# A four-layer cross-attention kernel: the latent layers' output projection in whole fp32 operands

## The chip, the core and the metric

The kernel runs on one core of one Trainium2 chip. Its time is the device time of one execution in microseconds (us); lower is better. A core has five engines that run their own instruction streams and meet at semaphores: TensorE (PE; its weight loads are listed as PEld), VectorE (DVE), ScalarE (ACT), GpSimd (POOL) and SyncE (SP), which here issues all DMAs.

## What is computed

Four attention layers run one after the other on 16 batches of a 128 x 512 fp32 activation. Layers 0 and 3 are the "latent" kind, layer 1 is grouped-query attention, layer 2 is cross attention. All but layer 1 end in an MLP of width 2048. A latent layer, cut to what matters (here `h` is the context and the latents together, 16 heads of 32):

```python
q  = latents @ q_w + q_b
kv = h @ kv_w + kv_b
attn = softmax(where(mask, q @ k.T / 32, -inf))
attn_out = attn @ v                          # (16, 128, 512)
attn_out = attn_out @ out_w + out_b + residual   # the output projection
out = rmsnorm(attn_out, postnorm_w)
out = gelu(out @ mlp_w1 + mlp_b1) @ mlp_w2 + mlp_b2
return out + residual
```

The change is in the line marked as the output projection, in layers 0 and 3.

## The kernel before

**Split operands.** Dense products are made from fp32r operands (a rounded fp32 type that TensorE takes as it is). Each operand is held twice: `hi` is the value rounded to fp32r, `lo` is the fp32r of value minus `hi`. `three_passes` (recorded as L326) multiplies lo x hi, hi x lo and hi x hi into the same bank of PSUM, so one product of 128 rows of contraction takes three matmuls. A few products take plain fp32 operands instead: attention times values in `pe_attend` (L497), and the transposes (L467, L361, L521).

**Where operands lie.** On-chip memory is seen through two sets of tensors over the same bytes: `plain_low`, `plain_high`, `plain_work` in fp32, and `rounded_low`, `rounded_high`, `rounded_work` in fp32r. Slots 0 to 7 are "low", 8 to 15 "high". Layer 0's output weight has slots 6 and 7 (hi and lo, low) and its heads slot 15 (high); layer 3's has slots 14 and 15 (high) and its heads slot 7 (low). So in a trace the output projection of layer 0 is `banks<-rounded_low,rounded_high` and that of layer 3 `banks<-rounded_high,rounded_low`, each 192 matmuls.

**Weights.** SP loads a weight in tiles of 128 x 512 (`load_tile`) into a double buffer, and POOL splits each with `split_tile`: a cast to `hi` (L315), then a subtraction to `lo` (L317). Layer 0's four output-weight tiles are split right at the start; layer 3's are the last four of 16 that POOL splits during the last group of layer 2's MLP.

**Banks.** PSUM has 8 banks. Four hold scores or MLP sums. The other four are a ring (`begin`): every result takes the next one and waits until the reader of four results ago has counted its `evac` semaphore.

**A latent layer.** Batches go in 8 pairs `p`, each with four rounds `k` (batch k % 2, heads half k // 2). The orders on the engines are written out by hand in `pe_latent`, `act_latent`, `dve_latent`, `pool_latent`, `sp_latent`. For a middle pair PE runs: scores(p,1), transposes of the probabilities of (p,0), **out(2p-1)**, attend(p,0), keys 0 and 1 of pair p+1, scores(p,2), transposes(p,1), queries 0, attend(p,1), values, scores(p,3), transposes(p,2), keys 2, attend(p,2), keys 3, scores(p+1,0), transposes(p,3), **out(2p)**, attend(p,3), queries, values. out(15) stands alone behind the last pair. So each of the two layers has 16 output projections ("out blocks"): eight out(2p), seven out(2p-1), and out(15).

**Around an out block.** `pe_attend` leaves a round's heads in a ring bank. `act_heads` (L745) writes bias plus value of two 128 x 128 blocks as `hi`; `dve_heads` (L1053) then writes the two `lo` blocks and frees the bank. `pe_out` waits for the bank's `evac` of the two rounds of its batch, and multiplies four blocks of heads (as weights) by the output weight (512 columns, moving). `dve_out` (L1150) adds it to the residual in `hidden`, then come statistics (L1135, L1137, L1140) on DVE, the root and the scaling on POOL (`pool_root`), and a store by SP. In layer 0 the keys of pair p+1 wait for that pair's inputs: ACT rounds them (`act_stage`, L809) after the exponentials of heads 0 and 1 of scores(p,1), DVE makes the `lo` part (`dve_stage`, L1109) and counts `xc_ready`.

Of the kernel before, what the change touches and what calls it, by code (L numbers as in the profile page):

```python
# [8 lines left out]
ACT = mybir.ActivationFunctionType  # L9
# [7 lines left out]
P = 128  # L17
B = 16
PAIRS = B // 2
D = 512  # L20
FB = D // P
# [7 lines left out]
LATENT, GQA, CROSS = "latent", "gqa", "cross"  # L29
# [33 lines left out]
def build(nc, ins, out):  # L63
# [9 lines left out]
    with ctx:  # L73
# [3 lines left out]
        def sem(name):  # L77
            return ctx.enter_context(nc.semaphore(name))

        C_KB = 76  # L80
        with nc.sbuf_tensor("plain_low", [P, 8 * 2048], F32) as plain_low, \
                nc.sbuf_tensor("plain_high", [P, 8 * 2048], F32) as plain_high, \
                nc.sbuf_tensor("plain_work", [P, C_KB * KB], F32) as plain_work:
            plain = [plain_low, plain_high, plain_work]
# [3 lines left out]
        def shaped(v, shape):  # L88
            names = "abcd"[:len(shape)]
            if len(shape) == 1:  # L90
                return v
            return v.rearrange(f"p ({' '.join(names)}) -> p {' '.join(names)}", **dict(zip(names[1:], shape[1:])))

        def work(t, at_kb, *shape):
            at, n = int(at_kb * KB), int(np.prod(shape))
            return shaped(t[2][:, at:at + n], shape)

        def slots(t, s, *shape):
            at, n = (s % 8) * 2048, int(np.prod(shape))
            return shaped(t[s // 8][:, at:at + n], shape)  # L100
# [35 lines left out]
        def prob(y):  # L136
            return [slots(plain, y.probs + h, 4, D) for h in range(2)]

        def prob_t(y):
            return work(plain, 36, 4, D) if y.kind == GQA else slots(plain, y.probs + 2, 4, D)  # L140

        def heads_t(y):
            return slots(rounded, 15 if y.kind == GQA else y.probs + 3, 2, 2, 4, P)

# [58 lines left out]
        raw_scaled, tile_hi, tile_split = sem("raw_scaled"), sem("tile_hi"), sem("tile_split")  # L203
# [9 lines left out]
        def bank(key):  # L213
            return PS[:, 4 + ring[key] % 4, :]

        def begin(pe, key):
            n = len(ring)
            ring[key] = n
            wait(pe, evac[n % 4], n // 4)
            return PS[:, 4 + n % 4, :]  # L220

        def filled_by(key):
            return filled[ring[key] % 4]

        def evac_of(key):
            return evac[ring[key] % 4]

        def wait_filled(eng, key):
            eng.wait_ge(filled[ring[key] % 4], ring[key] // 4 + 1)

        def wait_evac(eng, key):
            eng.wait_ge(evac[ring[key] % 4], ring[key] // 4 + 1)
# [10 lines left out]
        def col(y, i):  # L243
            return cols[:, y.n, i:i + 1]

        def of_round(y, k):
            return (k, 0) if y.kind == CROSS else (k % 2, k // 2)
# [24 lines left out]
        def attention_tiles(y, names):  # L272
            t = []
            a = ins[f"attention_w{y.n}"]
            if "kv" in names:
                for f in range(FB):
                    t.append((ins["attention_kv1"][f], 2 * P, W[10][:, f * 256:f * 256 + 256], W[10][:, 1024 + f * 256:1024 + f * 256 + 256], None))
            for name in [n for n in names if n != "kv"]:
                hi, lo = y.homes[name]
                for f in range(FB):  # L280
                    t.append((a[("qo" if y.kind == GQA else "kvqo").index(name), f], D, W[hi][:, f * D:(f + 1) * D], W[lo][:, f * D:(f + 1) * D],
                              y.scale if name == "q" else None))
            return t
# [23 lines left out]
        def split_tile(pool, key, i):  # L307
            n = first_tile[key] + i
            src, width, hi, lo, scale = tile_table[key][i]
            buf = raw[:, n % 2, 0:width]  # L310
            pool.wait_ge(raw_loaded[n % 2], 16 * (n // 2 + 1))
            if scale is not None:
                pool.tensor_scalar(buf, buf, scale, 1.0, ALU.mult, ALU.mult).then_inc(raw_scaled, 1)
                pool.wait_ge(raw_scaled, scale_order.index((key, i)) + 1)
            pool.tensor_copy(hi, buf).then_inc(tile_hi, 1)  # L315
            pool.wait_ge(tile_hi, n + 1)
            pool.tensor_tensor(lo, buf, hi.bitcast(F32), ALU.subtract).then_inc(tile_split, 1)  # L317
# [6 lines left out]
        def three_passes(pe, dst, lhs, rhs, first, last):  # L324
            for n, (i, j) in enumerate(((1, 0), (0, 1), (0, 0))):
                mm = pe.matmul(dst, lhs(i), rhs(j), start=first and n == 0, stop=last and n == 2, skip_group_check=True)  # L326
            return mm
# [131 lines left out]
        def pe_turn_probs(pe, y, p, k):  # L459
            R = y.round(p, k)  # L460
            pr = prob(y)[R % 2]
            for r in range(4):
                key = ("T", R, r)
                dst = begin(pe, key)
                pe.wait_ge(normed, 4 * R + r + 1)
                for t in range(4):
                    mm = pe.transpose(dst[:, t * P:(t + 1) * P], pr[:, r, t * P:(t + 1) * P], ident[:, :])  # L467
                mm.then_inc(filled_by(key), 1)

        def pe_attend(pe, y, p, k):  # L470
            R = y.round(p, k)
            b, s = of_round(y, k)
            pt = prob_t(y)
            key = ("O", R)
            dst = begin(pe, key)
            for r in range(4):
                wait_evac(pe, ("T", R, r))
            if y.kind == CROSS:
                pe.wait_ge(vc_loaded[p % 2], 16 * (p // 2 + 1))
            else:  # L480
                for i in range(4 if y.kind == LATENT else 1):
                    wait_evac(pe, ("V", y.n, p, i))
            n_blk = 4 if y.kind == CROSS else 2
            n_t = 4 // n_blk
            for i in range(n_blk):
                c = n_blk * s + i
                for t in range(n_t):
                    for r in range(4):
                        u = 4 * c + r
                        if y.kind == LATENT:  # L490
                            v = V_L[p % 2][:, 2 * t + b, 32 * u:32 * u + 32]
                        elif y.kind == GQA:
                            v = V_G[p % 2][:, 4 * b + r, t, :]
                        else:
                            v = V_C[p % 2][:, b, 32 * u:32 * u + 32]
                        at = (i * n_t + t) * P
                        mm = pe.matmul(dst[32 * r:32 * r + 32, i * P:(i + 1) * P], v, pt[:, r, at:at + P],  # L497
                                       start=t == 0, stop=t == n_t - 1, skip_group_check=True)
            mm.then_inc(filled_by(key), 1)

        def pe_out(pe, y, b):
            if b == 0:
                pe_weights(pe, y, "o")
            p = b // 2
            for k in range(y.per_pair):
                if of_round(y, k)[0] == b % 2:
                    wait_evac(pe, ("O", y.round(p, k)))
            key = ("out", y.n, b)
            dst = begin(pe, key)
            ot = heads_t(y)  # L510
            for f in range(FB):
                mm = three_passes(pe, dst, lambda h: ot[:, b % 2, h, f, :], lambda h: weight(y, "o", h, f, 0, D), f == 0, f == FB - 1)
            mm.then_inc(filled_by(key), 1)
# [222 lines left out]
        def act_heads(act, y, p, k):  # L736
            R = y.round(p, k)
            b, s = of_round(y, k)
            key = ("O", R)
            ot = heads_t(y)  # L740
            n_blk = 4 if y.kind == CROSS else 2
            wait_filled(act, key)
            for i in range(n_blk):
                c = n_blk * s + i
                last = act.activation(ot[:, b, 0, c, :], bank(key)[:, i * P:(i + 1) * P], ACT.Identity, bias=col(y, 8 + c))  # L745
            last.then_inc(hi_done, hi_count(key))

        def act_keys(act, y, p, i):
# [293 lines left out]
                dve_invert(dve, y, p, k)  # L1042

        def dve_heads(dve, y, p, k):
            R = y.round(p, k)
            b, s = of_round(y, k)
            key = ("O", R)
            ot = heads_t(y)
            n_blk = 4 if y.kind == CROSS else 2
            wait_hi(dve, key)  # L1050
            for i in range(n_blk):
                c = n_blk * s + i
                last = dve.scalar_tensor_tensor(out=ot[:, b, 1, c, :], in0=bank(key)[:, i * P:(i + 1) * P], scalar=col(y, 8 + c),  # L1053
                                                in1=ot[:, b, 0, c, :].bitcast(F32), op0=ALU.add, op1=ALU.subtract)
            last.then_inc(evac_of(key), 1)
# [913 lines left out]
```

## Time and profile before

| | |
|---|---|
| time, median of 2 runs | 2566.01 us (2565.93 to 2566.09) |
| the profiled execution's own time | 2566.45 us |
| its span, first to last instruction | 2564.5 us |
| PE busy | 2450.6 us (96%), 18464 matmuls |
| DVE / ACT / POOL busy | 1235.5 / 1085.5 / 1118.6 us (48 / 42 / 44%) |
| mean granted TensorE clock | 0.983 of full |
| HBM read, written | 136.22 MB, 58.72 MB: 76 GB/s over the span |

The profile is one execution. A row of a group gives the line of the source, engine, operation, what is written from what, the shape, the count, then busy time and mean length of one, and idle time before it with what ended it. Matmuls are pipelined: the length of one overlaps the next, so the cost of a matmul in a stream is the time of a run of them divided by their count, not its own length. The chain of work that ended last gives such runs. From the activations of the MLPs the stages are: layer 0 to 448 us, its MLP to 792, layers 1 and 2 to 1431, MLP to 1775, layer 3 to 2210, MLP to the end.

### The profile page before, as it was taken

The page shows a single profiled execution, that of the slowest core. Times are in us where ns is not written, and L with a number is a line of the kernel's source. Part 1 is how long each engine was busy: PE and PEld are TensorE (multiplying, and loading weights), DVE is VectorE, ACT ScalarE, POOL GpSimd, SP SyncE. Part 2 cuts the span into 40 slices and gives each one's busy share as a digit, 9 for nine tenths or more (in the row PEclk, how much of TensorE's full clock was granted, in tenths as well). Part 3 has the DMA queues.
Part 4 walks back from the last instruction along what each step waited for, and adds up shares of the span by engine and source line. Part 5 has one row for each costly group of instructions (what it writes and reads, how often), then busy time and mean ns, then how long its engine had stood idle before and what let it go on. Part 6 is the DMA issues. An engine that isn't in the chain of part 4 may idle for free.

```text
span 2564.5 us, 48767 instructions
## 1 busy us (share of the span) xinstructions
PE 2450.6 (96%) x18464; PEld 2052.2 (80%) x18464; DVE 1235.5 (48%) x3296; ACT 1085.5 (42%) x3712; POOL 1118.6 (44%) x1972
## 2 busy tenths in 40 slices
PE   7999998999999999998888999999999999899999
PEld 6888786888888878886777788888888888788887
DVE  4555655333234666766666442333455555432332
ACT  4555555111113777787676211111555555311111
POOL 2444435600043787878876740023344443730000
PEclk9999999999999999998998999999999999999999
DMA  4111222311034223223453320122022111320100
GB/s 162 59 59 59 96 63 67 95 50 50 1 98 136 74 106 120 90 102 124 137 168 120 116 96 1 50 84 77 26 84 66 51 42 59 116 87 1 50 33 17
DMA packets 106774, 198.07 MB, mean 77 GB/s; under 512 B 8304, under 2 KB 35632, under 8 KB 103600
## 3 DMA queue, kind: packets, MB, share of 16 engines
q1 hardware_dynamic: 106544, 194.97, 22.8%
q8 instruction: 149, 2.44, 0.4%
q14 instruction: 81, 0.66, 0.1%
HBM read 136.22 MB, written 58.72 MB: 76 GB/s over the span
## 4 chain that ended last, share of the span: by engine, by line
PE 79%; ACT 11%; DVE 5%; POOL 3%; issue 1%; DMA 1%; SPq 0%; DVEq 0%; POOLq 0%
PE banks L326 70%; ACT plain_high L731 5%; PE banks L467 5%; PE banks L497 3%; ACT plain_low L731 2%; POOL plain_high L1344 2%; ACT plain_work L796 1%; DVE stats L1135 1%; PE banks L521 1%; DVE rounded_work L1109 1%; ACT plain_work L715 1%; DMA plain_high<-attention_w 0%; DVE plain_work L1150 0%; DVE plain_high L1004 0%; ACT plain_low L715 0%
## 5 line engine op out<-in xcount | busy, mean ns | idle before, releaser
L326 PE MATMUL banks<-rounded_work,rounded_low 128*128 128x512 f32 (+1 forms) x2688 | 536.8, 356 | 18.9 <-DVE rounded_low L1168 9.5
L326 PEld LDWEIGHTS banks<-rounded_work,rounded_low 128*128 128x128 f32 x2688 | 447.4, 200 | 84.4 <-issue 12.3
L982 ACT ACTIVATE plain_work<-banks,columns 128x512 f32<-128x512 f32 x192 | 132.4, 690 | 870.8 <-PE banks L326 870.8
L326 PE MATMUL banks<-rounded_work,rounded_high 128*128 128x512 f32 (+1 forms) x2400 | 480.9, 354 | 1.0 <-DMA rounded_work<-ctx_split 0.6
L326 PEld LDWEIGHTS banks<-rounded_work,rounded_high 128*128 128x128 f32 x2400 | 394.3, 190 | 66.7 <-issue 5.8
L1344 POOL TENSOR_SCALAR plain_high<-plain_high,inv_sum 128x128 f32<-128x128 f32 (+1 forms) x768 | 296.1, 408 | 324.2 <-DVE inv_sum L1026 323.8
L1320 DVE CAST rounded_work<-plain_work 128x512 fp32r<-128x512 f32 x192 | 105.7, 551 | 683.2 <-ACT plain_work L982 672.5
L326 PE MATMUL banks<-rounded_low,rounded_work 128*128 128x512 f32 x1728 | 414.9, 391 | 0.0
L326 PE MATMUL banks<-rounded_high,rounded_work 128*128 128x512 f32 (+1 forms) x1728 | 390.2, 377 | 0.0
L326 PEld LDWEIGHTS banks<-rounded_low,rounded_work 128*128 128x128 f32 x1728 | 321.6, 188 | 68.6 <-issue 2.8
L326 PEld LDWEIGHTS banks<-rounded_high,rounded_work 128*128 128x128 f32 x1728 | 309.1, 188 | 60.6 <-issue 1.4
L1344 POOL TENSOR_SCALAR plain_low<-plain_low,inv_sum 128x128 f32<-128x128 f32 (+1 forms) x512 | 218.7, 448 | 283.1 <-DVE inv_sum L1026 283.0
L1490 POOL TENSOR_TENSOR plain_work<-plain_work 128x512 f32<-128x512 f32 x48 | 66.6, 1418 | 609.4 <-DMA plain_work<-x 417.1
L731 ACT ACTIVATE plain_low<-banks,neg_max 128x128 f32<-128x128 f32 (+1 forms) x512 | 208.9, 456 | 27.9 <-DVE neg_max L1008 27.9
L731 ACT ACTIVATE plain_high<-plain_high,neg_max 128x128 f32<-128x128 f32 x512 | 198.1, 392 | 33.5 <-DVE neg_max L1004 33.5
L1008 DVE TENSOR_REDUCE neg_max<-banks 128x2 f32<-128x512 f32 (+1 forms) x320 | 204.9, 683 | 14.0 <-PE banks L456 13.9
L467 PE MATMUL banks<-ident,plain_high 128*128 128x128 f32 x1024 | 139.1, 284 | 28.4 <-POOL plain_high L1344 22.5
L1322 DVE TENSOR_TENSOR rounded_work<-plain_work,rounded_work 128x512 fp32r<-128x512 f32 x192 | 162.0, 844 | 6.6
L467 PEld LDWEIGHTS banks<-ident,plain_high 128*128 128x128 f32 x1024 | 112.5, 143 | 47.7 <-issue 25.8
L1026 DVE RECIPROCAL inv_sum<-row_sum 128x4 f32<-128x4 f32 (+1 forms) x224 | 41.7, 187 | 219.8 <-ACT plain_high L731 124.9
L326 PEld LDWEIGHTS banks<-rounded_work 32*128 32x128 f32 x3072 | 101.3, 185 | 43.0 <-issue 41.1
L326 PE MATMUL banks<-rounded_work 32*128 32x256 f32 (+1 forms) x3072 | 123.1, 289 | 9.7 <-DVE rounded_work L1080 7.0
(106 smaller groups left out, 3120.6 us busy)
## 6 DMA issues: line engine op xcount, KB each, us to landing
plain_work<-x SPq DMA_DIRECT2D x96, 256.0 KB, 3.2
plain_work<-mlp_w SPq DMA_DIRECT2D x96, 256.0 KB, 2.7
rounded_work<-ctx_split SPq DMA_DIRECT2D x16, 1024.0 KB, 6.0
u<-plain_work SPq DMA_DIRECT2D x48, 256.0 KB, 2.7
plain_work<-u SPq DMA_DIRECT2D x12, 1024.0 KB, 7.1
x<-plain_work SPq DMA_DIRECT2D x48, 256.0 KB, 2.3
plain_work<-attention_w SPq DMA_DIRECT2D x44, 256.0 KB, 2.7
ctx_split<-rounded_work SPq DMA_DIRECT2D x8, 1024.0 KB, 5.6
```

The costliest lines, as they stand in the source:

```text
L326: mm = pe.matmul(dst, lhs(i), rhs(j), start=first and n == 0, stop=last and n == 2, skip_group_check=True)
L467: mm = pe.transpose(dst[:, t * P:(t + 1) * P], pr[:, r, t * P:(t + 1) * P], ident[:, :])
L497: mm = pe.matmul(dst[32 * r:32 * r + 32, i * P:(i + 1) * P], v, pt[:, r, at:at + P], start=t == 0, stop=t == n_t - 1, skip_group_check=True)
L521: mm = pe.transpose(dst[:, r * P:(r + 1) * P], u_nat[:, r, f * P:(f + 1) * P], ident[:, :])
L731: last = act.activation(pr[:, r, part], pr[:, r, part] if gqa else PS[:, r, part], ACT.Exp, scale=-1.0 if gqa else 1.0, bias=neg_max[:, R ...
L982: act.activation(gelu[:, j % 2, :], bank(key), ACT.Gelu_apprx_tanh, bias=col(y, 28 + j)).then_inc(evac_of(key), 1)
L1008: dve.tensor_reduce(neg_max[:, R % 2, r, 0:y.segs], src.rearrange("p (g n) -> p g n", g=y.segs), AX.X, ALU.max, negate=True).then_inc(maxe ...
L1026: dve.reciprocal(inv_sum[:, R % 2, 2 * half:2 * half + 2, 0:y.segs], row_sum[:, R % 2, 2 * half:2 * half + 2, 0:y.segs]).then_inc(inverted, 1)
L1320: dve.tensor_copy(G[:, j % 4, 0, :], gelu[:, j % 2, :]).then_inc(g_hi, 1)
L1322: dve.tensor_tensor(G[:, j % 4, 1, :], gelu[:, j % 2, :], G[:, j % 4, 0, :].bitcast(F32), ALU.subtract).then_inc(g_ready, 1)
L1344: last = pool.tensor_scalar(part, part, inv_sum[:, R % 2, r, g:g + 1], 1.0, ALU.mult, ALU.mult)
L1490: last = pool.tensor_tensor(res[:, r, :], res[:, r, :], wide_bias, ALU.add)
```

## The change

In the two latent layers the output projection takes plain fp32 operands. `pe_out` issues one fp32 matmul for each of the four blocks instead of three fp32r ones. `act_heads` writes the heads as fp32 and frees the bank itself; `dve_heads` returns at once. `split_tile` copies the weight tile in two halves (the second one counts the semaphore that the subtraction counted) and makes no `lo`. Layers 1 and 2 are as before.

```diff
+        def full_heads_t(y):
+            return slots(plain, y.probs + 3, 2, 4, P)
 ...
             for name in [n for n in names if n != "kv"]:
                 hi, lo = y.homes[name]
                 for f in range(FB):
+                    if y.kind == LATENT and name == "o":
+                        t.append((a["kvqo".index(name), f], D, slots(plain, hi, 2048)[:, f * D:(f + 1) * D], None, None))
+                        continue
 ...
         def split_tile(pool, key, i):
+            if lo is None:
+                half = width // 2
+                pool.tensor_copy(hi[:, 0:half], buf[:, 0:half]).then_inc(tile_hi, 1)
+                pool.tensor_copy(hi[:, half:width], buf[:, half:width]).then_inc(tile_split, 1)
+                return
             pool.tensor_copy(hi, buf).then_inc(tile_hi, 1)
             pool.wait_ge(tile_hi, n + 1)
             pool.tensor_tensor(lo, buf, hi.bitcast(F32), ALU.subtract).then_inc(tile_split, 1)
 ...
             ot = heads_t(y)
+            if y.kind == LATENT:
+                full, w = full_heads_t(y), slots(plain, y.homes["o"][0], FB, D)
+                for f in range(FB):
+                    mm = pe.matmul(dst, full[:, b % 2, f, :], w[:, f, :], start=f == 0, stop=f == FB - 1, skip_group_check=True)
+                mm.then_inc(filled_by(key), 1)
+                return
             for f in range(FB):
                 mm = three_passes(pe, dst, lambda h: ot[:, b % 2, h, f, :], lambda h: weight(y, "o", h, f, 0, D), f == 0, f == FB - 1)
 ...
-                last = act.activation(ot[:, b, 0, c, :], bank(key)[:, i * P:(i + 1) * P], ACT.Identity, bias=col(y, 8 + c))
+                to = full_heads_t(y)[:, b, c, :] if y.kind == LATENT else ot[:, b, 0, c, :]
+                last = act.activation(to, bank(key)[:, i * P:(i + 1) * P], ACT.Identity, bias=col(y, 8 + c))
+            if y.kind == LATENT:
+                last.then_inc(evac_of(key), 1)
+                return
             last.then_inc(hi_done, hi_count(key))
 ...
         def dve_heads(dve, y, p, k):
+            if y.kind == LATENT:
+                return
```

On PE, around an out block of layer 0 in the order of issue (rows of the program: names as above, shape and count; L497 is attend, L467 the transposes). Before:

```order
L326 MATMUL banks<-rounded_work 128x256 x24
L456 MATMUL banks<-plain_work,ones_row 128x2x128 x4
L467 MATMUL banks<-ident,plain_high 128x128 x16
L326 MATMUL banks<-rounded_low,rounded_high 128x512 x12
L497 MATMUL banks<-plain_high,plain_work 32x128 x16
L326 MATMUL banks<-rounded_work,rounded_low 128x256 x24
```

and now, with the lines of the changed kernel:

```order
L337 MATMUL banks<-rounded_work 128x256 x24
L467 MATMUL banks<-plain_work,ones_row 128x2x128 x4
L478 MATMUL banks<-ident,plain_high 128x128 x16
L525 MATMUL banks<-plain_low,plain_high 128x512 x4
L508 MATMUL banks<-plain_high,plain_work 32x128 x16
L337 MATMUL banks<-rounded_work,rounded_low 128x256 x24
```

The twelve matmuls of an out block are four; nothing else changes place. On DVE, from an out block's sum to the next exponentials' maxima, before:

```order
L1150 TENSOR_TENSOR plain_work<-banks,plain_work 128x512
L1135 BN_STATS stats<-plain_work 128x6
L1137 BN_AGGR moments<-stats 128x2
L1140 SCALAR_TENSOR_TENSOR spread<-moments 128x1
L1053 SCALAR_TENSOR_TENSOR rounded_high<-banks,columns,rounded_high 128x128 x2
L1080 SCALAR_TENSOR_TENSOR rounded_work<-banks,columns,rounded_work 128x256 x2
```

and now:

```order
L1173 TENSOR_TENSOR plain_work<-banks,plain_work 128x512
L1158 BN_STATS stats<-plain_work 128x6
L1160 BN_AGGR moments<-stats 128x2
L1163 SCALAR_TENSOR_TENSOR spread<-moments 128x1
L1103 SCALAR_TENSOR_TENSOR rounded_work<-banks,columns,rounded_work 128x256 x2
```

The two instructions that made the `lo` heads (old L1053) are gone there, as they are after every attend of layers 0 and 3.

## Rows read from the trace of the kernel before

**Rows 1.** The page, part 1: busy us, share of span, count.
```profile
PE 2450.6 (96%) x18464; PEld 2052.2 (80%) x18464; DVE 1235.5 (48%) x3296; ACT 1085.5 (42%) x3712; POOL 1118.6 (44%) x1972
```

**Rows 2.** The page, part 4: shares of the chain that ended last, by engine.
```profile
PE 79%; ACT 11%; DVE 5%; POOL 3%; issue 1%; DMA 1%; SPq 0%; DVEq 0%; POOLq 0%
```

**Rows 3.** Busy time by stage: layer 0, its MLP, layer 3.
```profile
core 0: us, PE busy (x) PEld busy (x) DVE busy (x) ACT busy (x) POOL busy (x), PEclk, DMA share, GB/s
26.00:448.30 422.30, 401.49 (x3727) 333.11 (x3726) 237.57 (x483) 226.60 (x734) 187.53 (x350) 0.98 0.21 66
448.30:791.60 343.30, 343.30 (x1540) 284.95 (x1540) 103.68 (x150) 51.37 (x76) 100.57 (x98) 1.00 0.19 61
...
1774.60:2210.40 435.80, 422.69 (x3902) 351.82 (x3901) 241.46 (x498) 226.35 (x744) 184.91 (x347) 0.99 0.19 63
```

**Rows 4.** Groups by form, whole program, PE and PEld: xcount | busy us, mean ns.
```profile
L326 PE MATMUL banks<-rounded_low,rounded_high 128*128 128x512 f32 x192 | 48.3, 400 | 1.5 <-issue 1.5
...
L497 PE MATMUL banks<-plain_high,plain_work 128*32 128x128 f32 x1024 | 34.9, 277 | 3.7 <-DVE plain_high L1013 2.2 <-issue 1.5
...
L326 PEld LDWEIGHTS banks<-rounded_low,rounded_high 128*128 128x128 f32 x192 | 35.2, 190 | 8.6 <-issue 1.8
...
L497 PEld LDWEIGHTS banks<-plain_high,plain_work 128*32 128x32 f32 x1024 | 26.3, 110 | 13.2 <-issue 12.2
```

**Rows 5.** Chain that ended last, pair 3 of layer 0: start us, us, what.
```profile
202.94 0.60 ACT plain_high L715
...
205.85 0.96 ACT rounded_work L809
...
207.97 1.23 DVE rounded_work L1109
...
209.24 6.70 PE banks L326 x48
215.94 0.13 PE banks L456 x4
216.07 1.90 PE banks L467 x16
217.96 2.87 PE banks L326 x24
220.84 1.01 PE banks L497 x32
...
230.50 2.75 PE banks L326 x12
```

**Rows 6.** Waits of PE in layer 0: us in total, times, longest us.
```profile
PE banks L326 <- DVE rounded_work L1109: 9.3, 7, 1.7
```

**Rows 7.** Timeline of PE and DVE, last pair of layer 0: out(13) and what follows.
```profile
410.72 0.84 PE L326 MATMUL banks<-rounded_low,rounded_high 128*128 128x512 f32 x3
411.50 1.08 PE L497 MATMUL banks<-plain_high,plain_work 128*32 128x128 f32 x32
...
424.52 3.81 PE L467 MATMUL banks<-ident,plain_high 128*128 128x128 f32 x16 [3.37 <-POOL plain_high L1344]
```

**Rows 8.** Chain that ended last, last pair of layer 0.
```profile
412.47 0.70 DVE plain_work L1150
...
416.58 2.89 DMA plain_work<-mlp_w
```

**Rows 9.** Timeline of layer 3's last pair: out(13) and its sum.
```profile
2171.53 2.99 PE L326 MATMUL banks<-rounded_high,rounded_low 128*128 128x512 f32 x12
...
2175.43 0.69 DVE L1150 TENSOR_TENSOR plain_work<-banks,plain_work 128x512 f32<-128x512 f32 x1
```

**Rows 10.** Timeline between the last attend of layer 0 and out(15).
```profile
441.08 0.62 ACT L745 ACTIVATE rounded_high<-banks,columns 128x128 fp32r<-128x128 f32 x2 [4.36 <-PE banks L497]
...
441.85 0.60 DVE L1053 SCALAR_TENSOR_TENSOR rounded_high<-banks,columns,rounded_high 128x128 fp32r<-128x128 f32 x2
...
442.56 1.17 PE L326 MATMUL banks<-rounded_low,rounded_high 128*128 128x512 f32 x4 [1.54 <-issue]
```

**Rows 11.** Groups on DVE in layer 0, the heads' second parts.
```profile
L1053 DVE SCALAR_TENSOR_TENSOR rounded_high<-banks,columns,rounded_high 128x128 fp32r<-128x128 f32 x64 | 19.2, 342 | 0.3 <-ACT rounded_high L745 0.3
```

**Rows 12.** POOL's subtraction (L317) by tile: ns min/median/max, starts, forms.
```profile
L317 POOL TENSOR_TENSOR rounded_low<-plain_work,rounded_low x68: 1262/1288/3266, 17.7 to 2247.2; 128x512 fp32r<-128x512 f32 x68
```

## The prediction

> **What bounds the kernel now.** I read the page's busy times first: PE is busy 96% of the span, no other engine over 48% [rows 1]. The chain that ended last agrees: 79% of it is PE [rows 2]. Busy time by stage then says where the change falls. The two latent layers hold 422 and 436 us, of which PE lacks about 21 and 13 us; in the MLP behind layer 0 it lacks nothing [rows 3]. So in these layers a longer or shorter PE block is a longer or shorter kernel, except where PE waits anyway right behind it. Work taken from DVE or POOL is worth something only where PE waits for just that work. The chain of one pair of layer 0 shows both: long unbroken runs of PE, and one place where the chain leaves PE for ACT and DVE [rows 5].
>
> **What an out block costs now.** Its twelve fp32r matmuls of 512 columns, between transposes and attend, take 2.75 us in the chain [rows 5], 229 ns each. Its group has 192 of them in layer 0, so 16 blocks [rows 4]; layer 3 has the same number under swapped names. That is 32 blocks and 88 us in all.
>
> **What it costs afterwards.** The trace has no plain fp32 matmul of 512 columns, so this price is built from the nearest rows.
> - How many instructions: the program issues 16 matmuls in an attend, and the trace has 32 MATMULs for it [rows 5]. So one plain fp32 matmul runs as two MATMULs, each with its own weight load (1024 of each in layer 0 for 32 rounds [rows 4]). An out block becomes 8 MATMULs.
> - How long each: the 32 MATMULs of an attend, 128 columns each, take 1.01 us. They use 32 weight columns each and lie four abreast in the array, so they are eight steps of some 109 ns with a bit of filling (1.01 / 8 = 126 at most). The fp32r stream of 24 with 256 columns takes 2.87 us, 120 ns each [rows 5]. A plain fp32 MATMUL of 128 columns thus needs about what an fp32r one of 256 needs: it streams its columns twice. The transposes say the same: 16 of 128 columns in 1.90 us, 119 ns each with the draining of the last one in it [rows 5]. And the mask's four bf16 matmuls of 256 columns, four abreast, take 0.13 us [rows 5], as long as one such step of 128 fp32 columns.
> - So a MATMUL of 512 plain columns should cost four times a step of 128. Below: two fp32r streams less their fixed part. fp32r goes from 120 ns at 256 columns to 229 at 512, 109 ns for 256 more columns, so 1024 columns take 4 x 109 = 436 ns, or 447 with the 11 ns that the 256-column row has over 109. Above: twice the whole 229, 458 ns. I take 436 to 447, rounded to 440, as the plain matmuls of the attend show no more than 109 for their step. The block: 8 x 440 = 3.52 us, 0.77 us more than 2.75.
> - The Trainium skill ("FP8 and Floating Point Precision", TensorE Precision Notes) says that true fp32 is four passes through the array. By that rule and the 229 ns of an fp32r pass a block would be 16 x 229 = 3.66 us, 0.91 more instead of 0.77; summed as below that would give 2586 instead of 2583. The rows on the attend agree with the four passes.
>
> **Where the 0.77 us is hidden.** In layer 0, out(2p-1) is followed by attend(p,0) and then by the keys of the next pair, and these wait for the inputs: 7 waits of 9.3 us in all, the longest 1.7 [rows 6]. The longest is pair 0, which has no out before it; the other six (p = 1 to 6) have 1.27 us each. The chain there runs ACT's copy of the transposes, exponentials, L809, DVE's L1109 [rows 5], and needs nothing of the out block. So the six blocks grow into a wait of 1.27 us and cost nothing; half a microsecond of it stays. A seventh is out(13) of layer 0: what follows it waits at the next transposes 3.37 us for POOL [rows 7], whose chain goes through DVE's sum L1150 of out(13) at 412.47 [rows 8], while the block ends at 410.72 + 0.84 = 411.56 [rows 7]. The slack of 0.91 covers 0.77. An eighth is the same block in layer 3: it ends at 2171.53 + 2.99 = 2174.52, DVE takes it up at 2175.43 [rows 9], slack 0.91. The other 24 blocks (16 - 7 and 16 - 1) have no such wait near them and stand on PE's path.
>
> **What is saved.** DVE loses 128 instructions of 342 ns, 44 us [rows 11], layer 3 as layer 0. No PE wait in the steady pairs is for them, so this cover costs nothing and brings nothing, with one exception in each layer: out(15) waits for the last heads. There ACT works 0.62 us from 441.08, DVE from 441.85 to 442.45, PE starts at 442.56 [rows 10]. Without DVE, PE starts about 0.1 us after ACT, near 441.8: 0.75 us less, 1.5 us for both layers. ACT's own work keeps its size and frees the bank earlier. POOL loses eight subtractions of 1.29 us [rows 12] and copies in two pieces. Layer 0's are made at 16 us and read after pair 0; layer 3's under the MLP, where PE has no gap. Without these covers they would be worth 10 us; with them nothing. SP issues the same DMAs.
>
> **Sum.** 24 x 0.77 = 18.5, less 1.5, is +17.0 us. On the profiled execution (2566.45, of it span 2564.5) that is 2583.4; that run lies 0.4 above the median of 2566.01, so the median should be about 2583.
>
> **Rivals.**
> - *One pass of the columns in each MATMUL.* If a plain fp32 MATMUL of 512 columns cost what an fp32r one does, the block would be 8 x 229 = 1.83 us, 0.92 less. The 109 ns at 128 columns would then be a floor and not streaming. For it: both fp32 rows in the trace have only 128 columns, and a load of 128 weights is 190 ns long itself [rows 4]. Against it: an attend loads only 32 weight columns at a time (110 ns long [rows 4]) and is no quicker a step than a transpose. The six waits of layer 0 would eat their gain, as would the two of out(13): 24 x 0.92 + 1.5 = 23.6 less, 2542 us. It is faster than before, by 0.9%. The block decides it: below 2.75 us the kernel gains.
> - The Trainium skill ("Perfetto Trace Analysis", Engine Utilization) halves the peak output rate for FP32_LOW_HIGH, which read for a whole fp32 product would be 4 x 2 x 229 = 1.83 us a block, just this rival. Read for each of the two MATMULs it is my forecast. No row of 512 plain columns tells the two apart.
> - *Weight loads come to light.* A block's eight fp32 loads of 128 weights are 190 ns each [rows 4] and lie under the running matmul today. If the second MATMUL of each pair could not have its weights ahead, four loads show: 4 x 0.19 = 0.76 more, a block of 4.28 us. That is +1.53 on 24 blocks, 0.26 on the six with 1.27 us of wait, about 0.6 on the other two, less 1.5: +38, 2604. If all eight show, +2.29: 55 + 6.1 + 2.7 - 1.5 = +62, 2628, 2.4% slower. Against both: in the attend, with as many loads as matmuls, the step stays at 109.
> - *Nothing to be seen.* If all blocks were covered as the eight are, the time would be 2565. PE's idle time in layer 3 is 13 us [rows 3] and nearly all in its first and last pair, so this has next to no chance.
>
> **How the numbers follow.** The forecast has 0.80, one pass 0.07, half of the loads 0.07, all of them 0.04, no effect 0.02. The forecast's own range is 436 to 458 ns a MATMUL, with or without slack of a few us: 2577 to 2590. The range given is 2574 to 2605: it takes in the case of half the loads and leaves out 0.13. Below 2% (51 us, about what a measurement of this kernel can tell from no change) lie all cases but the last of the loads: same 0.95, slower 0.04, faster 0.01.
>
> **What would show it.** The groups by form should list 256 MATMULs of 512 columns that read `plain_low` and `plain_high`, 128 in each layer, each clearly longer than the 400 ns of now. The chain should have them as x8 in 3.5 us; 1.8 is the first rival, 4.3 or 5.0 the second. The wait for L1109's successor should fall from 1.27 to about 0.5 six times. Layer 0's stretch should be some 6 us longer (9 x 0.77 - 0.75), layer 3's some 11 (15 x 0.77 - 0.75), the rest unchanged. The gap ahead of out(15) should be 0.8 instead of 1.54. I am wrong if the six waits stay at 1.27 while layer 0 grows by 11: then the chain to L1109 does pass through the out block. I am also wrong if the clock, 0.98 and 0.99 in these stages [rows 3], falls with the fp32 blocks.

## The result, and the profile after

The changed kernel takes 2580.89 us (median of 2 runs, 2578.56 and 2583.21) against 2566.01, a ratio of 1.0061 with a 95% interval from 1.0044 to 1.0077: slower by 15 us, within the 2% that were called "same", inside the range given (2574 to 2605) and 2 us from its point (2583.0).

The page of the profiled execution (2578.56 us, span 2576.5), part 1 and the first row of part 4:

```profile
span 2576.5 us, 48383 instructions
...
PE 2469.8 (96%) x18336; PEld 2026.7 (79%) x18336; DVE 1190.9 (46%) x3168; ACT 1085.3 (42%) x3712; POOL 1110.2 (43%) x1972
...
PE 79%; ACT 11%; DVE 5%; POOL 3%; issue 1%; DMA 1%; SPq 0%; DVEq 0%; POOLq 0%
```

Against [rows 1, 2]: PE has 128 matmuls fewer and is busy 19 us longer, DVE has lost 128 instructions and 44.6 us, POOL 8 us, ACT nothing, and the shares of the chain are what they were. The engine that bounds the kernel got more to do; those that got less did not bound it.

Busy time by stage: layer 0, its MLP, layer 3 (as [rows 3]):

```profile
core 0: us, PE busy (x) PEld busy (x) DVE busy (x) ACT busy (x) POOL busy (x), PEclk, DMA share, GB/s
26.00:451.20 425.20, 409.82 (x3658) 319.89 (x3657) 218.09 (x417) 224.75 (x726) 185.38 (x347) 0.98 0.20 66
451.20:794.50 343.30, 343.30 (x1540) 285.03 (x1540) 102.83 (x150) 51.36 (x76) 100.96 (x98) 1.00 0.20 61
...
1776.40:2222.40 446.00, 434.26 (x3838) 341.15 (x3838) 222.36 (x434) 226.19 (x745) 185.46 (x347) 0.99 0.19 61
```

Layer 0 ends 2.9 us later and layer 3 is 10.2 us longer (446.0 against 435.8). The 2.9 are less than layer 0 costs, because this execution reaches its first attend 1.8 us sooner (48.9 us instead of 50.7); from the first to the last attend layer 0 grows by 4.8 us, from 389.3 to 394.1. The MLP has the same 343.3 us. The granted clock is 0.98, 1.00 and 0.99 as before.

The new group, from the groups by form:

```profile
L525 PE MATMUL banks<-plain_high,plain_low 128*128 128x512 f32 x128 | 58.2, 598 | 0.8 <-issue 0.8
...
L525 PE MATMUL banks<-plain_low,plain_high 128*128 128x512 f32 x128 | 57.7, 593 | 0.8 <-issue 0.8
```

and its weight loads in layer 0, from the view of the line (ns min/median/max, first and last start):

```profile
L525 PEld LDWEIGHTS banks<-plain_low,plain_high x128: 186/190/192, 84.7 to 447.4; 128*128 128x128 f32 x128
```

Eight MATMULs a block, 128 in each layer, as the attend's two for one had said. The chain of work that ended last, pair 3 of layer 0 and the start of the next, stands beside [rows 5]:

```profile
206.14 0.95 ACT rounded_work L830
...
208.26 1.23 DVE rounded_work L1132
...
209.53 6.65 PE banks L337 x47
216.18 0.13 PE banks L467 x4
216.31 1.90 PE banks L478 x16
218.21 2.87 PE banks L337 x24
221.08 1.01 PE banks L508 x32
...
240.38 3.44 PE banks L525 x8
243.82 1.01 PE banks L508 x32
```

The out block is 3.44 us where it was 2.75: +0.69. One MATMUL of 512 plain columns costs 430 ns in the stream, one of fp32r 229. Everything around it (1.90, 2.87, 1.01) is the same to the hundredth.

The waits of PE in layer 0, to be held against [rows 6]:

```profile
PE banks L337 <- DVE rounded_work L1132: 5.2, 7, 1.7
```

Pair 0 keeps its 1.7 us, so the other six have 3.5 us, 0.58 each, where they had 1.27.

### The profile page after: what moved, and what is told of

Its sections match the earlier page's. It is cut to its first block, busy times and chain, and to the rows that moved or that the text cites. A ratio compares the mean times of both kernels' runs of the same rounds, so it can differ in the third digit from the quotient of the medians.

```text
span 2576.5 us, 48383 instructions
## 1 busy us (share of the span) xinstructions
PE 2469.8 (96%) x18336; PEld 2026.7 (79%) x18336; DVE 1190.9 (46%) x3168; ACT 1085.3 (42%) x3712; POOL 1110.2 (43%) x1972
## 4 chain that ended last, share of the span: by engine, by line
PE 79%; ACT 11%; DVE 5%; POOL 3%; issue 1%; DMA 1%; SPq 0%; DVEq 0%; POOLq 0%
PE banks L337 67%; ACT plain_high L748 5%; PE banks L478 5%; PE banks L525 3%; PE banks L508 3%; ACT plain_low L748 2%; POOL plain_high L1367 2%; ACT plain_work L817 1%; DVE stats L1158 1%; PE banks L538 1%; DVE rounded_work L1132 1%; ACT plain_work L732 1%; DVE plain_high L1025 1%; DVE plain_work L1173 0%; DMA plain_high<-attention_w 0%
## 5 line engine op out<-in xcount | busy, mean ns | idle before, releaser
L478 PE MATMUL banks<-ident,plain_low 128*128 128x128 f32 x768 | 104.7, 287 | 27.6 <-DVE plain_work L1173 9.1
```

## Experiments

In the results below, "before" is the kernel before, timed beside each experiment on the same chip; its runs lie between 2562 and 2573 us. So a single execution says little about 5 us, and where I can I read a stretch within one layer from the trace rather than the whole time. Between traces of the same code, pairs 1 to 6 of a layer repeat to some tenths of a us; pair 0 of layer 0 differs by up to 0.8 us and the last pair of a layer by up to 1.5.

**The changed kernel again**, no edit.

> The changed kernel once more, unedited, timed over more rounds, since its two executions lay 4.6 us apart (2578.6 and 2583.2) and the trace of the shorter one accounts for 12.0 us of span. If the cost is what the trace shows of the out blocks (24 blocks on the path at 0.69 us more each, less 0.75 us twice at out(15), so +15.1), the median stands 15 us over before, +-2. If the extra 4.6 us of the longer execution is the rule, it stands 17 to 19 over; if it is the exception, 12 to 14.

2580.82 us (5 runs, 2580.06 to 2583.16), ratio 1.0059, interval 1.0045 to 1.0072: 14.8 us over a before of 2566.04. That fits the first of the three cases best; the interval, 11.5 to 18.5 us, does not rule out the other two.

**The kernel before again**, no edit.

> The kernel before, unedited, for a second trace of it. The first trace of it and that of the changed kernel differ by 1.8 us before the first attend and by 2.5 us within the cross layer, where both kernels run the same program. If these are differences from one execution to the next (arrival of the first loads, DMA), this trace of before differs from the first one by amounts of that kind at the same places, with a ratio of 1.000 in time. If they belong to the change, this trace agrees with the first of before within 0.3 us at every attend.

2566.94 us (10 runs), ratio 1.0001 (0.9989 to 1.0012), but the profiled one has a span of 2569.4 us instead of 2564.5. The two traces of one program agree within 0.2 us at every attend of layer 0. Then they part in three steps: the second one is 1.8 us later behind layers 1 and 2, 3.3 at the first attend of layer 3, and 5.0 at its last one. So differences of some us come from one execution to the next. The two traces of the changed kernel show it as well: from layer 0's last attend to layer 3's first one took 1.1 us less than before, the other 1.6 more. The -2.5 us in the cross layer are not the change's.

The spread goes with TensorE's granted clock. Of these ten executions the six up to 2568.1 us have a mean of 0.985 or 0.986, the next one (2568.7) has 0.983 and the three above 2571 have 0.981; 0.004 of 2565 us is 10 us, as much as the whole spread. The trace shows one of the steps directly: from 1775 to 1800 us, where layer 3 starts, the granted clock is 1.00 in the first trace and 0.93 in the second, which is 1.7 us, about the step from 1.8 to 3.3.

The 1.8 us at the very start of the changed kernel's trace I did not see between these two. All eleven other traces reach the first attend sooner than the first one of before: the five whose clock is 1.00 over the first 48 us by 2.4 to 3.0 us, the five with 0.96, among them this one, by 0.2 to 1.0; the changed kernel's first trace, with 0.96 too, by 1.8. What else decides it is open, and so is what brings the clock down in one execution and not in another. No run changed the clock by itself, so that it is the cause of the spread is likely and not shown.

**Layer 0 alone, layer 3 alone.** The conditions `y.kind == LATENT` of the change become `y.n == 0`, or `y.n == 3`:

```diff
-            if y.kind == LATENT:
+            if y.n == 0:
                 full, w = full_heads_t(y), slots(plain, y.homes["o"][0], FB, D)
```

> Whole fp32 operands in layer 0 alone; layer 3 as before. My theory: seven of its 16 out blocks grow into waits, nine are on the path, so 9 x 0.69 - 0.75 = +5.5 us over before. Rival, that all blocks count: 16 x 0.69 - 0.75 = +10.3 us. Rival, that the time follows only the sum over both layers by some other effect (clock, a slower mode of the array around fp32): half of what both layers cost, +7.5.

> Whole fp32 operands in layer 3 alone; layer 0 as before. My theory: out(13) grows into slack, 15 blocks are on the path, 15 x 0.69 - 0.75 = +9.6 us over before. Together with layer 0 alone it makes +15.1. If layer 3 had the same waits as layer 0, or if the layers' shares were equal for another reason, it would cost as much as layer 0 alone.

Layer 0 alone: 2572.47 us, ratio 1.0023 (1.0013 to 1.0033), +5.9 us with 3.3 to 8.5; 16 blocks on the path would be +10.3, which is outside. Layer 3 alone: 2576.92, ratio 1.0039 (1.0025 to 1.0052), +10.0 us with 6.4 to 13.3. The same sixteen blocks cost 6 us in one layer and 10 in the other, and the sum is the cost of both within the intervals.

The rival of +7.5 for each lies inside both intervals, so the times do not exclude it; the traces do. From the first to the last attend, layer 0 grows from 389.3 to 395.1 us in the first of the two, layer 3 from 383.0 to 393.5 in the second. From the first attend to the last one of pair 6, so without the last pair, layer 3 grows by 9.3 us in the run of layer 3 alone and by 9.0 and 9.3 in the two traces of the changed kernel, where 13 blocks on the path make 13 x 0.69 = 9.0; layer 0 grows by 4.2 us in the run of layer 0 alone and by 4.7 and 5.0 in the changed kernel, where 7 x 0.69 = 4.8 are due. That 5.8 is so close to the 5.5 of eight blocks is in part luck: out(14) of layer 0 takes 4.64 us in that trace, at half the clock for a part of it, and 3.60 in the changed kernel.

**Only the blocks with a wait behind them; only the others.** In the kernel before, three more fp32r matmuls (0.69 us, the surcharge of the fp32 block) in layer 0's out blocks, the odd or the even ones:

```diff
             ot = heads_t(y)
+            if y.n == 0 and b % 2 and b < B - 1:
+                three_passes(pe, dst, lambda h: ot[:, b % 2, h, 0, :], lambda h: weight(y, "o", h, 0, 0, D), True, False)
             for f in range(FB):
```

> The kernel before, with the seven out blocks out(1), out(3) to out(13) of layer 0 made longer by three more fp32r matmuls (the first three passes are made twice, the sum starts anew), so by 3 x 0.229 = 0.69 us each, the surcharge of the fp32 block. My theory: all seven grow into waits that are there anyway; from the first to the last attend of layer 0 (389.3 us in before) nothing is added, the six waits before the next pair's keys fall from 1.27 to 0.58 us, and the time is that of before. Rival, that the blocks' length reaches the chain behind the wait: +4.8 us in layer 0.

> The same three added matmuls, in the eight out blocks out(0), out(2) to out(14) of layer 0 instead. My theory: these stand on PE's path, 8 x 0.69 = +5.5 us from the first to the last attend of layer 0 (389.3 us in before), the six waits stay at 1.27 us. Rival, that out(2p) has slack too: less than 3 us.

Seven odd blocks longer: 2565.99 against 2565.66, ratio 0.9996 (0.9987 to 1.0005), and 389.2 us from the first to the last attend of layer 0 instead of 389.3. Eight even blocks longer: 2572.45, ratio 1.0022 (1.0013 to 1.0031), +5.6 us with 3.3 to 8.0, and 395.0 us in layer 0, +5.7. The waits of PE, pairs 1 to 6 of layer 0, odd blocks longer and then even ones:

```profile
PE banks L326 <- DVE rounded_work L1111: 3.5, 6, 0.6
```
```profile
PE banks L326 <- DVE rounded_work L1111: 7.6, 6, 1.3
```

Work of 0.69 us in front of the wait comes out of it, six times 1.27 becomes six times 0.58; elsewhere it is paid in full. The rival, that the block's length reaches the chain behind the wait, is out.

**VectorE's heads kept.** The changed kernel, in which DVE again writes a second part (into a quarter of the slot that nobody reads) and frees the bank:

```diff
         def dve_heads(dve, y, p, k):
-            if y.kind == LATENT:
-                return
 ...
             wait_hi(dve, key)
+            if y.kind == LATENT:
+                full, spare = full_heads_t(y), slots(plain, y.probs + 3, 4, 4, P)
+                for i in range(n_blk):
+                    c = n_blk * s + i
+                    last = dve.scalar_tensor_tensor(out=spare[:, 2 + b, c, :], in0=bank(key)[:, i * P:(i + 1) * P], scalar=col(y, 8 + c),
+                                                    in1=full[:, b, c, :], op0=ALU.add, op1=ALU.subtract)
+                last.then_inc(evac_of(key), 1)
+                return
```

> The changed kernel, but VectorE still makes the second part of the heads of the latent layers (into a spare quarter of the slot that nobody reads) and frees the bank, as before. It takes back what the change saved beside TensorE. My theory: the gap ahead of out(15) goes from 0.79 back to about 1.5 us in both layers and nothing else moves: +1.5 us over the changed kernel. Rival, that the relief of VectorE (44 us busy) hides more: +3 us or more, with new waits of PE on the heads in the steady pairs.

2581.53 us, ratio 1.0062 (1.0049 to 1.0076), against 1.0059 of the changed kernel: too close to be told apart in time, as 1.5 us had to be. The chain in layer 0's last pair tells it, first of the changed kernel, then of this one:

```profile
442.97 1.01 PE banks L508 x32
443.98 0.79 issue
444.77 2.38 PE banks L525 x5
```
```profile
441.80 1.01 PE banks L508 x32
442.81 1.54 issue
444.35 1.96 PE banks L525 x4
```

0.79 against 1.54 us between the last attend and out(15) is all that the relief of DVE was worth in that layer; in layer 3 this gap is 1.54 us again too. The steady pairs have the same six waits of 0.58 us, and from pair 0's last attend to pair 6's it is 310.8 us in the changed kernel and 310.9 in this one.

**Half the columns, twice the matmuls.** Each fp32 matmul of the changed kernel in two of 256 columns:

```diff
                 for f in range(FB):
-                    mm = pe.matmul(dst, full[:, b % 2, f, :], w[:, f, :], start=f == 0, stop=f == FB - 1, skip_group_check=True)
+                    for half in range(2):
+                        part = slice(256 * half, 256 * half + 256)
+                        mm = pe.matmul(dst[:, part], full[:, b % 2, f, :], w[:, f, part], start=f == 0 and half == 0, stop=f == FB - 1, skip_group_check=True)
```

> The changed kernel with each fp32 matmul of 512 columns cut into two of 256: 16 MATMULs a block instead of 8. If a plain fp32 MATMUL streams its columns twice, one of 256 columns takes about 216 ns and the block stays near 3.44 us (16 x 216 = 3.46): the time of the changed kernel within 1 us. If there is a fixed part of a MATMUL (109 ns at 128 columns partly a floor), each takes more, up to 230: 16 x 230 = 3.68, +0.24 a block, +6 us. If weight loads can't be hidden under 256 columns, more than that.

2581.40 us, ratio 1.0061 (1.0048 to 1.0075). The block in its chain:

```profile
239.35 3.46 PE banks L527 x16
```

Sixteen MATMULs with sixteen weight loads take 3.46 us, 216 ns each, against 3.44 for eight. The price is in the columns, with about 2 ns for a MATMUL more: 109, 216 and 430 ns for 128, 256 and 512 columns are one line. Weight loads of 190 ns stay hidden even under 216.

**The wait itself.** If six blocks hid in a wait of 1.27 us, then the wait was worth 1.27 us before any change. In layer 0 ScalarE's rounding of the next pair's inputs goes one place ahead, in front of the exponentials of head 1; once in the kernel before and once in the changed one:

```diff
             if turned:
                 act_probs(act, of or y, *turned, 2)
+            if y.n == 0:
+                between()
             if k is not None:
                 act_exp(act, y, p, k, 1)
-            between()
+            if y.n:
+                between()
```

> The kernel before, with one step moved: in layer 0 ScalarE rounds the next pair's inputs one place earlier, ahead of the exponentials of heads 1 (0.91 us) instead of behind them. My theory of the wait that hid six blocks: it is the chain copy, exponentials, rounding, VectorE's second part; 0.8 us of VectorE's own wait for ScalarE goes, the six PE waits fall from 1.27 to about 0.45 us and pair 0's from 1.7 to 0.9, so 5 to 6 us less than before (2560). Rival, that the exponentials made later hold up the scores' banks or GpSimd's scaling: no gain, or new waits at the transposes.

> The changed kernel with the same step moved. The fp32 blocks need 0.69 us of each wait of 1.27; with the wait shortened by 0.8 there is only 0.45 left to hide in. My theory: PE's wait there is gone (0 to 0.1 us), but each of the six blocks now costs the rest, so the gain is 0.58 a pair, 3.5 us, and 0.8 in pair 0: about 4 us under the changed kernel and 11 above the kernel before. If cover and wait were independent, the gain would be the 5 to 6 us of the kernel before.

The kernel before with this step: 2558.88 us, ratio 0.9968 (0.9956 to 0.9980), 7 to 8 us faster and the fastest of all kernels here. The changed kernel with it: 2575.50, ratio 1.0035 (1.0023 to 1.0048), 9 us over before and some 6 under the changed kernel. Waits and chain of the first of the two, layer 0:

```profile
PE banks L326 <- DVE rounded_work L1112: 2.1, 6, 0.4
```
```profile
195.59 1.29 DVE neg_max L1011 x2
196.88 0.60 DVE plain_high L1016
197.48 1.20 DVE neg_max L1011 x2
198.67 0.60 DVE plain_high L1016
199.27 2.28 DVE rounded_work L1112 x2
201.55 0.04 issue
201.60 6.67 PE banks L326 x48
```

The six waits went from 1.27 to 0.36 us, a bit more than expected, and what stays of them is now DVE's own work, with no step of ACT in it. Pairs 1 to 6 took 306.9 us from attend to attend and take 301.4 (6 x 0.92). In the changed kernel they go from 310.8 to 306.9, 0.65 a pair rather than 0.91, and PE no longer waits there at all in these six pairs. So cover and wait are one thing: what one uses up, the other can't give. The whole gain came out larger than I had put it (7 us by the medians, 8 by the ratio, instead of 5 to 6; in the changed kernel some 5 to 6 instead of 4): in the kernel before, layer 0 from its first to its last attend is 8.0 us shorter, of which 5.5 are the six pairs, and 2.5 are pair 0. Its wait is gone as a whole (it was 1.7); the other 0.8 go with the clock, which is 0.86 from 48 to 60 us in this trace and 0.72 in that of before, so they are likely no gain of the move. In the changed kernel pair 0 keeps 0.6 of its 1.7 us.

## Why the prediction was right

- **PE bounds the latent layers, the others' relief is worth nothing.** Right. DVE lost 44.6 us busy, POOL 8, and 0.75 us a layer came of it, with 0.79 left of the 1.54 in [rows 10] where 0.8 was said.
- **Eight MATMULs a block, each streaming its columns twice.** Right in number and kind; the rivals of one pass (1.83 us a block) and of exposed weight loads (4.3 or 5.0) are out by the row of 3.44 us. The Trainium skill ("FP8 and Floating Point Precision", TensorE Precision Notes) gives true fp32 four passes through the array, and the trace agrees in count; at 229 ns a pass, that of fp32r, it would be 3.66 us, and 3.44 were measured. The halved rate for FP32_LOW_HIGH in the Trainium skill ("Perfetto Trace Analysis", Engine Utilization) agrees only if it is read for each of the two MATMULs: 430 ns against 229.
- **The size of a MATMUL.** A bit off: 440 ns were put, 430 measured, so 0.77 us for the block's growth was 0.69. The step was "1024 columns take 4 x 109 = 436 ns, or 447 with the 11 ns that the 256-column row has over 109", rounded to 440. The measured steps of 109, 216 and 430 ns rise by 107 ns for each 128 plain columns, with a part of 2 ns that does not grow. Four times the attend's 109 counts that part four times, which is 6 of the 10 ns. The 109 between the two fp32r rows is too high by the same 2 ns, because 229 is the mean over a whole block; in the long fp32r streams of the trace these matmuls start 227 ns apart. The other 4 ns are the rounding towards the 447, that is towards the part that fp32r pays beyond its columns and the plain MATMUL does not.
- **Where it is hidden.** Right: the timeline of the changed kernel has the wait ahead of the next pair's keys at 0.58 us six times (1.27 - 0.69; about 0.5 was said), and out(13) ends just before DVE takes it up:

```profile
411.54 3.60 PE L525 MATMUL banks<-plain_low,plain_high 128*128 128x512 f32 x8
...
415.36 0.69 DVE L1173 TENSOR_TENSOR plain_work<-banks,plain_work 128x512 f32<-128x512 f32 x1
```

It ends at 415.14, 0.22 us before DVE's sum; the slack in [rows 7, 8] was 0.91. In layer 3 the same block ends at 2186.11 and the sum starts at 2186.32. From the start of out(13) to the start of the transposes behind the wait for POOL it is 15.95 us before and 15.70 now in layer 0, 15.82 and 15.63 in layer 3: the longer block did not push them back. The odd and even blocks made longer show the same in layer 0 with the operands untouched.
- **The sum.** With 0.69 for 0.77 it is 24 x 0.69 - 1.5 = +15.1 us; 14.9 and 14.8 were measured. By layer: 9 x 0.69 - 0.75 = 5.5 and 15 x 0.69 - 0.75 = 9.6; 5.9 and 10.0 measured for each alone, their intervals some 2.6 and 3.5 us to either side. The stretches of the changed kernel's own trace were said to grow by some 6 and 11 us; layer 3's grew by 10.2, layer 0's by only 2.9, as its start came 1.8 us sooner and its last pair grew by 0.1 us instead of 0.69.
- **The profiled execution** grew only by 12.0 us of span. The rest lies in places that differ between two traces of one program too: the start and the stretch between the two layers. That the median of only two executions comes within 0.2 us of 15.1 is in part luck, as executions of one kernel lie up to 10 us apart; the repetition with its interval of 11.5 to 18.5 us is the better number.
- **The clock.** Right: 0.98 and 0.99 in the two layers before and after, so the fp32 blocks did not bring it down.

## What to carry to other kernels

Count the passes of the bounding engine first: trading three fp32r passes for one fp32 matmul is four passes for three, and nothing that it saves on idle engines pays for that. Then walk the blocks one by one and ask what PE waits for next behind each: eight of 32 equal blocks cost nothing here, because the next step waited on a chain that did not pass through them. Such a wait can also be cheap to fix: moving one step of ScalarE ahead of another gained 7 to 8 us, about half of what the whole change lost, in a kernel that looked bound by PE alone.

## What the runs showed of the hardware

- A plain fp32 MATMUL streams in 109, 216 and 430 ns for 128, 256 and 512 columns. An fp32r one takes 120 and 229 ns for 256 and 512, so 11 and 13 ns more than a plain one of half its columns. I had not expected the fixed part to be on the fp32r side. Why it is there no run shows. It does not go on downwards as a line: 192 fp32r matmuls of 128 columns in layers 1 and 2 (L326 `banks<-rounded_high,rounded_work`) start 110 to 114 ns apart, hardly less than those of 256. So for fp32r a floor near 110 ns, as the first rival supposed it for plain fp32, does show; that the attend's 109 is no such floor but streaming is shown by the 216 and 430 ns that lie on one line with it.
- Weight loads of 190 ns lay under MATMULs of 216 ns and added at most the 2 ns above.
- Executions of one and the same kernel spread over some 10 us (2562 to 2573), and the longer ones have the lower mean granted clock: 0.981 to 0.983 above 2569.5 us, 0.983 to 0.986 below, in 69 executions of the kernel before. The steps lie in layers 1 and 2, at the start of layer 3 and in its last pair. A change of 0.2% needs many runs, or the trace of a single layer read beside its clock.
